# Attention whose short transpositions are done for two heads in one go, and earlier in their step

## The chip, the core and the metric

The kernel runs on one core of a Trainium2 chip. The time is the device time of one execution in microseconds (us). Before the change it is 2401.09 us, the median of 3 runs (2400.51 to 2401.67). The engines are named as the profile names them: PE is TensorE (matrix products and transpositions), PEld its weight loads, ACT is ScalarE, DVE is VectorE, POOL is GpSimd and SP is SyncE, which here issues the transfers.

## The reference

One transformer layer on `x` of shape (2, 1024, 512), in float32. Only the attention bears on the change:

```python
q = rope(hidden @ Wq.T)        # 32 heads of 128, per token
k = [k_c, rope(k_r)]           # 8 key/value heads, from low-rank projections
v = (c_kv @ Wupv.T)            # 8 heads of 128
scores = where(causal, q @ k.T / sqrt(128), -1e9)
attn = softmax(scores, axis=-1)
out = (attn @ v) @ Wo.T        # four query heads share one key/value head
x = layernorm(x + out)
# then a gated feed-forward layer with 4-bit weights, and a second layernorm
```

## The kernel before, in words

Every float32 product is done as three products of a high and a low part (`PASSES`), so each operand is kept as a pair: ACT copies the high part, DVE or POOL subtracts it to get the low part.

The program has three stages: projections of keys, values and latents for all tokens; attention (from 235 to about 2012 us of the span); the feed-forward layer. The attention stage makes 16 turns, one for each pair of a batch entry and a key/value head. Turn 0 is written out ("first"), turns 1 to 14 are a hardware loop ("loop"), turn 15 is written out ("last"), and a short "end" follows.

A turn has 32 steps, and 32 cells: cell c stands for query tile i = c // 4 (128 queries) and head h = c % 4 of the four query heads. In step s:

- PE computes the scores of cell s (`scores`): i+1 key tiles of 128 columns, into one of two PSUM buffers `b_sps`; 3 products for tiles 0 to 3, 6 narrower ones for tiles 4 to 7.
- DVE applies mask and scale and finds the maximum (L1250), into one of four slots of `b_sc` in SBUF. ACT takes the exponential with the row sum (L1026). Two steps later DVE starts its step with the reciprocal of the sum (L1258), and ACT multiplies by it (`normalise`, L1032; it raises `norm_done`).
- Three steps later (`LAG`) PE transposes the cell's probabilities, 128x128 at a time, in pieces of up to four key tiles, into one of two PSUM buffers `b_tps` (`transposes`, L1536). ACT copies the high part of the piece to `b_pt` (`hi_pt`, L1047), DVE subtracts for the low part (`lo_pt`, L1268; it raises `pt_lo`, which frees the PSUM buffer for the piece after next).
- Between these PE does "fill" work in slices of single products: values times probabilities of a query tile (`pv`), output projection (`wo`), and the queries of later cells (`q0`, `q1`). `FILL` and `ROOM` say which and how many products a step takes; `SHARES` cuts a step's fill into shares around the pieces, and `PE_ORDER`, `ACT_ORDER`, `DVE_ORDER` say in which order an engine does the jobs of a step ("0" and "1" are the first and second piece).

In the loop's part between steps 3 and 15 PE does scores, piece 0, fill; from step 16 on it does scores, a share of fill, piece 0, a share, piece 1, the last share. Cells of tiles 0 to 3 have one piece of 1 to 4 key tiles; cells of tiles 4 to 7 have a piece of 4 and a second one of 1 to 4 key tiles: 48 pieces a turn. Each engine works strictly in its own order; a wait on a semaphore holds all that stands behind it.

Two more jobs matter below. A `wo` product writes to one of two PSUM banks, and the next job of the same bank waits until DVE has added the result to `b_ys` (`add_y`, L1279), which DVE does at the start of the step after the product ended. And in steps 22, 26 and 30 of turns 0 to 14 DVE unpacks a piece of the feed-forward weights (L1296 to L1306) at the end of its step.

Of the kernel before, what the change touches and what calls it, by code (L numbers as in the profile page):

```python
# [25 lines left out]
ALU = mybir.AluOpType  # L26
ACT = mybir.ActivationFunctionType
# [3 lines left out]
GQ = HEADS // KV  # L31
# [22 lines left out]

def pieces(c):

    i = c // GQ
    first = c if i < 4 else 16 + 2 * (c - 16)
    out = [(first, 0, min(4, i + 1))]
    if i >= 4:  # L60
        out.append((first + 1, 4, i - 3))
    return out


PIECES = 48

# [31 lines left out]
def part_of(step):  # L98

    return (step >= LAG) + (step >= 16) + (step >= 24)  # L100
# [17 lines left out]

SHARES = ((1,), (0, 1), (1, 1.25, 1))


# [211 lines left out]
def layer(nc, x, xT, wqT, wkrT, wdkT, wupkT, wupvT, woT, w13p, s13p, w2p, s2p, cosT, sinT, shifts,  # L333
# [5 lines left out]
    with ExitStack() as ctx:  # L339
# [109 lines left out]
        def thru(c):  # L449

            return pieces(c)[-1][0] + 1 if c >= 0 else pieces(c + CELLS)[-1][0] + 1 - PIECES

# [475 lines left out]
        def _(act):  # L928
# [106 lines left out]
            def hi_pt(it, c, which):  # L1035
                i, h = c // GQ, c % GQ
                for n, j0, nj in pieces(c)[which:which + 1]:
# [9 lines left out]
                    nc.scalar.activation(pt[:, u % PT_UNITS, HI, 0:nj, h * P:(h + 1) * P], tps[n % 2][:, 0:nj],  # L1047
                                         ACT.Copy)\
                        .then_inc(pt_hi, 1)
# [86 lines left out]

            for _ in range(60):
                act.sem_inc(placed, 1)
# [27 lines left out]
        def _(dve):  # L1166
# [93 lines left out]
            def lo_pt(it, c, which):  # L1260
                i, h = c // GQ, c % GQ
                for n, j0, nj in pieces(c)[which:which + 1]:
# [5 lines left out]
                    nc.vector.tensor_tensor(pt[:, u, LO, 0:nj, h * P:(h + 1) * P], tps[n % 2][:, 0:nj],  # L1268
                                            pt[:, u, HI, 0:nj, h * P:(h + 1) * P], ALU.subtract).then_inc(pt_lo, 1)

# [195 lines left out]
        def _(pe):  # L1466
# [64 lines left out]
            def transposes(it, c, piece):  # L1531
                n, j0, nj = piece
                pe.wait_ge(norm_done, CELLS * it + c + 1)
                pe.wait_ge(pt_lo, PIECES * it + n + 1)
                for j in range(nj):
                    last = nc.tensor.transpose(tps[n % 2][:, j], sc[:, c % S_RING, (j0 + j) * P:(j0 + j + 1) * P],  # L1536
                                               ident[:])
                last.then_inc(t_done, 1)
# [149 lines left out]
            def turn_of(it, turn):  # L1688
                for step in range(CELLS):
# [11 lines left out]
                    shares = cut(parts, SHARES[len(ts)])  # L1701
                    for job in (0, 1, "scores") if step == 0 else PE_ORDER[part_of(step)]:
                        if job == "scores":
# [114 lines left out]
```

## Time and profile before

| | us |
|---|---|
| median of 3 runs | 2401.09 |
| the profiled execution | 2403.64 |
| its span, first to last instruction | 2401.9 |
| PE busy | 2376.6 (99%), 12028 products and transpositions |
| PEld busy | 1993.7 (83%) |
| ACT busy | 1619.4 (67%), 3221 instructions |
| DVE busy | 1428.4 (59%), 3780 instructions |
| POOL busy | 579.1 (24%) |
| mean granted TensorE clock | 0.997 of full |
| attention stage, 235 to 2012 us: PE, ACT, DVE busy | 1768.1, 1460.8, 1198.9 of 1777 |
| PE's share of the chain that ended last | 94% |

The profiled execution took 1.7 us more than its span, and 2.6 us more than the median of the runs. The records of matrix products overlap, since the engine is pipelined, so a busy PE is no proof that nothing waits: a wait is seen as a product that starts later than the rhythm of its neighbours.

### The profile page before, as it was taken

To read this page: it belongs to the slowest core of one execution; us is meant where nothing else is said; L and a number is where in the kernel's file an instruction comes from. 1 tells how busy PE (TensorE), PEld (TensorE's weight loads), DVE (VectorE), ACT (ScalarE), POOL (GpSimd) and SP (SyncE) were. 2 spreads that over 40 slices of the span, in tenths; PEclk is the share of its full clock that TensorE was granted. 3 is DMA by queue.
4 is the path that set the end of the run, shared out by engine and by line. 5 is a ranking of instruction groups with operands and counts; after the bars stand their busy time and mean duration, and the time that the engine had idled before them with its cause. 6 is when DMAs were issued, how large, how long until landed. Compare 5 with 4: busy or idle time off the path is not lost.

```text
span 2401.9 us, 41145 instructions
## 1 busy us (share of the span) xinstructions
PE 2376.6 (99%) x12028; PEld 1993.7 (83%) x12028; DVE 1428.4 (59%) x3780; ACT 1619.4 (67%) x3221; POOL 579.1 (24%) x453
## 2 busy tenths in 40 slices
PE   9999999999999999999999999999999999999998
PEld 7888888888888888888888888888888888888886
DVE  5334666676767666666667666766676675242332
ACT  4223878788888878888878888887878885122211
POOL 3002323233332323232323233232323220000000
PEclk9999999999999999999999999999999999999999
DMA  8868444344353544344434434344444445320110
GB/s 271 289 212 295 139 134 139 127 140 144 133 174 103 175 131 153 127 140 136 152 127 140 137 133 160 120 170 120 161 134 140 132 141 196 131 71 35 52 35 18
DMA packets 133239, 340.24 MB, mean 142 GB/s; under 512 B 13312, under 2 KB 30720, under 8 KB 122624
## 3 DMA queue, kind: packets, MB, share of 16 engines
q1 hardware_dynamic: 133184, 339.53, 41.9%
q8 instruction: 31, 0.51, 0.1%
q14 instruction: 24, 0.20, 0.0%
HBM read 232.00 MB, written 111.67 MB: 143 GB/s over the span
## 4 chain that ended last, share of the span: by engine, by line
PE 94%; DVE 2%; ACT 2%; issue 1%; DMA 0%; POOL 0%; DVEq 0%; SPq 0%; ACTq 0%; POOLq 0%
PE b_ps L267 43%; PE b_sps L267 34%; PE b_tps L1536 10%; PE b_tps L1590 2%; PE b_ps L1590 2%; PE b_tps L267 2%; ACT b_sc L1026 1%; DVE b_ys L1279 0%; DVE b_wraw L1303 0%; DVE b_wraw L1300 0%; DMA b_xs<-xs_d 0%; ACT b_pt L1047 0%; PE b_sps L1545 0%; ACT b_sc L1032 0%; DVE b_pt L1268 0%
## 5 line engine op out<-in xcount | busy, mean ns | idle before, releaser
L1268 DVE TENSOR_TENSOR b_pt<-b_tps,b_pt 128x512 fp32r<-128x512 f32 (+3 forms) x768 | 426.8, 556 | 303.0 <-ACT b_pt L1047 300.0
L267 PE MATMUL b_sps<-b_kt,b_qs 128*128 128x512 f32 (+4 forms) x2304 | 497.2, 343 | 0.7 <-POOL b_qs L878 0.7
L1032 ACT ACTIVATE b_sc<-b_sc,b_rinv 128x896 f32<-128x896 f32 (+7 forms) x512 | 396.1, 774 | 126.5 <-DVE b_rinv L1258 121.1
L267 PEld LDWEIGHTS b_sps<-b_kt,b_qs 128*128 128x128 f32 x2304 | 403.1, 188 | 56.3 <-POOL b_qs L878 1.1
L267 PE MATMUL b_ps<-b_xs,b_wq 128*128 128x512 f32 x1536 | 442.0, 407 | 1.0 <-DMA b_xs<-xs_d 1.0
L1047 ACT ACTIVATE b_pt<-b_tps 128x512 fp32r<-128x512 f32 (+3 forms) x768 | 366.9, 478 | 105.6 <-PE b_tps L1536 103.9
L267 PE MATMUL b_ps<-b_pt,b_vt 128*128 128x512 f32 x1584 | 435.5, 402 | 0.3 <-DVE b_ys L1279 0.3
L267 PE MATMUL b_ps<-b_wo,b_ot 128*128 128x512 f32 x1536 | 425.5, 406 | 6.2 <-DVE b_ys L1279 6.2
L1026 ACT ACTIVATE b_sc<-b_sc,b_nmax 128x896 f32<-128x896 f32 (+7 forms) x512 | 395.6, 773 | 43.8 <-DVE b_nmax L1250 40.0
L1250 DVE CUSTOM_DVE_ANT_0 b_sc<-b_sps,b_mask 128x896 f32<-128x896 f32 (+7 forms) x512 | 386.4, 755 | 15.4 <-PE b_sps L267 15.3
L1536 PE MATMUL b_tps<-b_ident,b_sc 128*128 128x128 f32 x2304 | 374.3, 272 | 1.0 <-DVE b_pt L1268 1.0
L1536 PEld LDWEIGHTS b_tps<-b_ident,b_sc 128*128 128x128 f32 x2304 | 291.8, 140 | 75.5 <-issue 3.8
L267 PEld LDWEIGHTS b_ps<-b_pt,b_vt 128*128 128x128 f32 x1584 | 284.3, 188 | 49.0 <-DVE b_ys L1279 0.5
L267 PEld LDWEIGHTS b_ps<-b_wo,b_ot 128*128 128x128 f32 x1536 | 269.4, 189 | 53.3 <-DVE b_ys L1279 10.8
L267 PEld LDWEIGHTS b_ps<-b_xs,b_wq 128*128 128x128 f32 x1536 | 272.5, 189 | 49.1 <-issue 3.7
L878 POOL TENSOR_TENSOR b_qs<-b_qf,b_qs 128x512 fp32r<-128x512 f32 x124 | 160.3, 1293 | 434.4 <-ACT b_qs L1006 434.4
L267 PE MATMUL b_sps<-c_xs,c_up 128*128 128x512 f32 (+3 forms) x1056 | 247.7, 390 | 0.0
L267 PEld LDWEIGHTS b_sps<-c_xs,c_up 128*128 128x128 f32 (+1 forms) x1056 | 195.2, 185 | 43.7
L874 POOL TENSOR_TENSOR b_sw<-b_sw,b_sin 128x512 f32<-128x512 f32 x128 | 166.0, 1297 | 146.5 <-ACT b_sw L999 145.1
L1327 DVE TENSOR_TENSOR c_hb<-b_sps,c_hb 128x512 f32<-128x512 f32 (+1 forms) x44 | 30.4, 691 | 196.2 <-PE b_sps L267 189.6
L1232 DVE TENSOR_TENSOR b_qf<-b_ps,b_cos 128x512 f32<-128x512 f32 x128 | 88.5, 691 | 96.9 <-ACT b_sw L999 55.0
L887 POOL TENSOR_TENSOR b_wo<-b_wraw,b_wo 128x512 fp32r<-128x512 f32 x64 | 82.9, 1295 | 228.7 <-ACT b_wo L1020 228.7
(133 smaller groups left out, 2278.0 us busy)
## 6 DMA issues: line engine op xcount, KB each, us to landing
b_xs<-xs_d SPq DMA_DIRECT2D x32, 2048.0 KB, 9.2
b_ys<-y_d SPq DMA_DIRECT2D x128, 256.0 KB, 2.7
y_d<-b_ys SPq DMA_DIRECT2D x128, 256.0 KB, 3.0
k_d<-a_ks SPq DMA_DIRECT2D x32, 512.0 KB, 3.9
v_d<-a_vs SPq DMA_DIRECT2D x32, 512.0 KB, 3.0
b_kt<-k_d SPq DMA_DIRECT2D x64, 256.0 KB, 4.5
b_vt<-v_d SPq DMA_DIRECT2D x16, 1024.0 KB, 4.8
b_wraw<-in_wqT SPq DMA_DIRECT2D x64, 256.0 KB, 2.7
```

Source lines behind the costliest of these rows:

```text
L267: ins = nc.tensor.matmul(out, *every[n], start=(n == 0), stop=(n == len(every) - 1))
L874: nc.gpsimd.tensor_tensor(sw[:], sw[:], sinq[:, blk * TB:blk * TB + TB], ALU.mult).then_inc(sin_done, 1)
L878: nc.gpsimd.tensor_tensor(qs[:, blk, h, LO], qf[:], qs[:, blk, h, HI], ALU.subtract).then_inc(q_lo, 1)
L887: nc.gpsimd.tensor_tensor(wo[:, h, LO], wraw[:, h % 2], wo[:, h, HI], ALU.subtract).then_inc(w_lo, 1)
L1026: nc.scalar.activation(sc[:, slot, 0:w], sc[:, slot, 0:w], ACT.Exp, bias=nmax[:, slot:slot + 1], scale=-1.0, accum_out=rsum[:, slot:slot + ...
L1032: nc.scalar.activation(sc[:, slot, 0:w], sc[:, slot, 0:w], ACT.Copy, scale=rinv[:, slot:slot + 1])\
L1047: nc.scalar.activation(pt[:, u % PT_UNITS, HI, 0:nj, h * P:(h + 1) * P], tps[n % 2][:, 0:nj], ACT.Copy)\
L1232: nc.vector.tensor_tensor(qf[:], banks[bk], cosq[:, blk * TB:blk * TB + TB], ALU.mult)\
L1250: nc.vector.tensor_tensor_reduce(out=like_banks(sc[:, slot, 0:w], i), in0=both_banks(sps[c % 2], i), in1=like_banks(mask[:, S - w:S], i), ...
L1268: nc.vector.tensor_tensor(pt[:, u, LO, 0:nj, h * P:(h + 1) * P], tps[n % 2][:, 0:nj], pt[:, u, HI, 0:nj, h * P:(h + 1) * P], ALU.subtract) ...
L1536: last = nc.tensor.transpose(tps[n % 2][:, j], sc[:, c % S_RING, (j0 + j) * P:(j0 + j + 1) * P], ident[:])
L1590: last = nc.tensor.matmul(c_y[t], c_hs[0:w, f % 2, a, t * P:(t + 1) * P], c_w2[f][b][0:w], start=(f == 0 and k == 0), stop=(f == FT - 1 an ...
```

## The change

The pieces of one or two key tiles are no longer made for each head: the odd head's step transposes them for itself and the head before, so that a piece fills two or four of the four places of the PSUM buffer. This concerns query tiles 0 and 1 (their only piece) and 4 and 5 (their second piece). The even heads of tiles 0 and 1 have no piece of their own in their step. A turn has 40 pieces in place of 48, with the same 144 transpositions. In the odd heads' steps PE does the joined piece first, before the scores of that step; tile 4's and 5's steps with a single piece have the fill in one share behind that piece.

```diff
+JOINED = (0, 1, 4, 5)
+def all_pieces():
+    n, out = 0, []
+    for c in range(CELLS):
+        i, two = c // GQ, c % 2
+        mine = [] if i < 2 else [(1, 0, min(4, i + 1))]
+        if i in JOINED and two:
+            mine.insert(0, (2, 0, i + 1) if i < 2 else (2, 4, i - 3))
+        elif i >= 6:
+            mine.append((1, 4, i - 3))
+        out.append([(n + k, *piece) for k, piece in enumerate(mine)])
+        n += len(mine)
+    return out
...
+JOINED_SHARES = (None, (1,), (1, 1))
...
             def transposes(it, c, piece):
-                n, j0, nj = piece
+                n, cells, j0, nj = piece
                 pe.wait_ge(norm_done, CELLS * it + c + 1)
                 pe.wait_ge(pt_lo, PIECES * it + n + 1)
                 for j in range(nj):
-                    last = nc.tensor.transpose(tps[n % 2][:, j], sc[:, c % S_RING, (j0 + j) * P:(j0 + j + 1) * P],
-                                               ident[:])
+                    for e in range(cells):
+                        last = nc.tensor.transpose(tps[n % 2][:, j * cells + e],
+                                                   sc[:, (c - cells + 1 + e) % S_RING,
+                                                      (j0 + j) * P:(j0 + j + 1) * P], ident[:])
                 last.then_inc(t_done, 1)
...
-                    for job in (0, 1, "scores") if step == 0 else PE_ORDER[part_of(step)]:
+                    order = (0, 1, "scores") if step == 0 else PE_ORDER[part_of(step)]
+                    if cell and joined(cell[1]):
+                        order = (0, "scores", "fill", 1, "fill") if len(ts) == 2 else (0, "scores", "fill")
+                        shares = cut(parts, JOINED_SHARES[len(ts)])
+                    elif cell and not ts:
+                        order = ("scores", "fill")
+                    for job in order:
```

`hi_pt` and `lo_pt` take the joined piece as one instruction, 256 columns for each key tile; `thru`, which says how far the transpositions must be before a slot of `b_sc` is written again, counts the joined piece for both of its heads.

PE's order in the loop before, steps 3 and 4 (L1536 transposes, L267 with `b_sps` are the scores, with `b_ps` the fill; the register rows set up waits):

```order
365 L267 MATMUL b_sps<-b_kt,b_qs 128x256 x3
366 L1534 ISA
367 L1536 MATMUL b_tps<-b_ident,b_sc 128x128
368 L267 MATMUL b_ps<-b_xs,b_wq 128x512 x6
369 L1522 REGISTER_ALU
370 L267 MATMUL b_sps<-b_kt,b_qs 128x256 x3
371 L1534 REGISTER_ALU
372 L1536 MATMUL b_tps<-b_ident,b_sc 128x128
373 L267 MATMUL b_ps<-b_xs,b_wq 128x512
```

The same two steps after the change (here L1569 transposes and L289 is every product):

```order
347 L289 MATMUL b_sps<-b_kt,b_qs 128x256 x3
348 L289 MATMUL b_ps<-b_xs,b_wq 128x512 x6
349 L1566 ISA
350 L1569 MATMUL b_tps<-b_ident,b_sc 128x128 x2
351 L1554 REGISTER_ALU
352 L289 MATMUL b_sps<-b_kt,b_qs 128x256 x3
353 L289 MATMUL b_ps<-b_xs,b_wq 128x512
```

Cell 0's transposition left step 3, and both cells' stand ahead of step 4's scores, where cell 1's stood behind them.

PE's order in steps 22 and 23 of the loop before, up to the first `wo` product that needs the bank of the previous `wo`:

```order
488 L267 MATMUL b_sps<-b_kt,b_qs 128x384 x6
489 L267 MATMUL b_ps<-b_wo,b_ot 128x512 x4
490 L1534 REGISTER_ALU
491 L1536 MATMUL b_tps<-b_ident,b_sc 128x128 x4
492 L1634 ISA
493 L1635 REGISTER_ALU
494 L267 MATMUL b_ps<-b_xs,b_wq 128x512 x4
495 L1534 REGISTER_ALU
496 L1536 MATMUL b_tps<-b_ident,b_sc 128x128
497 L267 MATMUL b_ps<-b_xs,b_wq 128x512 x4
498 L1522 REGISTER_ALU
499 L267 MATMUL b_sps<-b_kt,b_qs 128x384 x6
```

After the change, the same place:

```order
454 L1569 MATMUL b_tps<-b_ident,b_sc 128x128 x2
455 L1554 REGISTER_ALU
456 L289 MATMUL b_sps<-b_kt,b_qs 128x384 x6
457 L289 MATMUL b_ps<-b_wo,b_ot 128x512 x4
458 L1668 ISA
459 L1669 REGISTER_ALU
460 L289 MATMUL b_ps<-b_xs,b_wq 128x512 x2
461 L1566 REGISTER_ALU
462 L1569 MATMUL b_tps<-b_ident,b_sc 128x128 x4
463 L289 MATMUL b_ps<-b_xs,b_wq 128x512 x6
464 L1554 REGISTER_ALU
465 L289 MATMUL b_sps<-b_kt,b_qs 128x384 x6
```

Two transpositions now stand ahead of step 22's scores, and the piece of four stands behind six products of fill where it stood behind four.

DVE's order in step 22 after the change; before, the two rows of L1299 were L1268 with 4x128 and then with 128 columns:

```order
468 L1280 ISA b_sc,b_nmax<-b_sps,b_mask 128x768
469 L1280 ISA b_nmax 128x1
470 L1299 TENSOR_TENSOR b_pt<-b_tps,b_pt 128x256
471 L1299 TENSOR_TENSOR b_pt<-b_tps,b_pt 128x4x128
472 L1326 ISA
473 L1332 TENSOR_TENSOR b_wraw<-b_wraw,d_sh 128x512
474 L1335 TENSOR_TENSOR b_wraw<-b_wraw,d_sh 128x512
475 L1337 REGISTER_ALU
476 L1338 TENSOR_TENSOR b_wraw<-b_wraw 128x512
477 L1288 RECIPROCAL b_rinv<-b_rsum 128x1
478 L1309 REGISTER_ALU
479 L1310 REGISTER_ALU
```

The small piece's low part stands ahead of the large one's, and the large one's now stands directly ahead of the unpacking and of `add_y` behind it.

## Rows read from the trace of the kernel before

**Rows 1.** Who TensorE's weight loads waited for: total us, times, longest.
```profile
PEld b_ps L267 <- DVE b_ys L1279: 11.3, 16, 0.7
```
**Rows 2.** Groups by form: busy us, mean ns of one, idle before.
```profile
L1047 ACT ACTIVATE b_pt<-b_tps 128x256 fp32r<-128x256 f32 x128 | 47.5, 371 | 30.4 <-PE b_tps L1536 30.4
L1047 ACT ACTIVATE b_pt<-b_tps 128x128 fp32r<-128x128 f32 x128 | 33.3, 260 | 0.3 <-PE b_tps L1536 0.3
```
**Rows 3.** Instructions in time, turn 6, steps 3 and 4: start us, us, what.
```profile
904.25 0.69 DVE L1268 TENSOR_TENSOR b_pt<-b_tps,b_pt 128x512 fp32r<-128x512 f32 x1
904.47 0.61 PE L267 MATMUL b_sps<-b_kt,b_qs 128*128 128x256 f32 x3
...
904.99 0.33 PE L1536 MATMUL b_tps<-b_ident,b_sc 128*128 128x128 f32 x1
...
905.38 0.69 DVE L1268 TENSOR_TENSOR b_pt<-b_tps,b_pt 128x512 fp32r<-128x512 f32 x1 [0.44 <-ACT b_pt L1047]
...
905.99 0.15 DVE L1258 RECIPROCAL b_rinv<-b_rsum 128x1 f32<-128x1 f32 x1
...
906.18 0.40 ACT L1032 ACTIVATE b_sc<-b_sc,b_rinv 128x128 f32<-128x128 f32 x1 [0.45 <-DVE b_rinv L1258]
...
906.55 0.52 PE L267 MATMUL b_sps<-b_kt,b_qs 128*128 128x256 f32 x3
```
**Rows 4.** The same, steps 4 to 6.
```profile
907.26 0.42 DVE L1250 CUSTOM_DVE_ANT_0 b_sc<-b_sps,b_mask 128x256 f32<-128x256 f32 x1
...
907.73 0.51 ACT L1026 ACTIVATE b_sc<-b_sc,b_nmax 128x256 f32<-128x256 f32 x1
...
908.53 0.27 PE L1536 MATMUL b_tps<-b_ident,b_sc 128*128 128x128 f32 x1
...
908.89 0.42 DVE L1250 CUSTOM_DVE_ANT_0 b_sc<-b_sps,b_mask 128x256 f32<-128x256 f32 x1
...
909.59 0.40 ACT L1032 ACTIVATE b_sc<-b_sc,b_rinv 128x128 f32<-128x128 f32 x1
...
910.49 0.52 PE L267 MATMUL b_sps<-b_kt,b_qs 128*128 128x256 f32 x3
```
**Rows 5.** The same, steps 22 and 23.
```profile
959.27 1.09 PE L267 MATMUL b_ps<-b_wo,b_ot 128*128 128x512 f32 x4
...
960.20 0.60 PE L1536 MATMUL b_tps<-b_ident,b_sc 128*128 128x128 f32 x4
...
960.83 0.60 ACT L1047 ACTIVATE b_pt<-b_tps 128x512 fp32r<-128x512 f32 x1 [1.05 <-PE b_tps L1536]
961.33 0.93 ACT L1026 ACTIVATE b_sc<-b_sc,b_nmax 128x768 f32<-128x768 f32 x1
...
961.46 0.69 DVE L1268 TENSOR_TENSOR b_pt<-b_tps,b_pt 128x512 fp32r<-128x512 f32 x1 [0.87 <-ACT b_pt L1047]
...
962.25 0.27 ACT L1047 ACTIVATE b_pt<-b_tps 128x128 fp32r<-128x128 f32 x1
...
962.75 0.68 DVE L1300 TENSOR_TENSOR b_wraw<-b_wraw,d_sh 128x512 int32<-128x512 int32 x1
...
964.88 0.67 DVE L1279 TENSOR_TENSOR b_ys<-b_ps,b_ys 128x512 f32<-128x512 f32 x1
...
965.60 0.73 PE L267 MATMUL b_ps<-b_wo,b_ot 128*128 128x512 f32 x2 [0.41 <-DVE b_ys L1279]
```
**Rows 6.** The same, turn 0, step 8.
```profile
245.38 0.69 PE L267 MATMUL b_sps<-b_kt,b_qs 128*128 128x384 f32 x3
245.47 0.49 ACT L1032 ACTIVATE b_sc<-b_sc,b_rinv 128x256 f32<-128x256 f32 x1
...
246.01 0.44 PE L1536 MATMUL b_tps<-b_ident,b_sc 128*128 128x128 f32 x2
```
**Rows 7.** The same, turn 15, step 26.
```profile
1976.11 0.94 ACT L1032 ACTIVATE b_sc<-b_sc,b_rinv 128x768 f32<-128x768 f32 x1 [1.26 <-DVE b_rinv L1258]
1976.27 1.38 PE L267 MATMUL b_sps<-b_kt,b_qs 128*128 128x448 f32 x6
```

More of the change, by code:

```diff
@@ L52, with joined @@
 UNITS = 12
-def pieces(c):
[L57 to L65, printed above, removed]
+JOINED = (0, 1, 4, 5)
[11 more added lines that the diff above has]
+    return out
+ALL_PIECES = all_pieces()
+PIECES = sum(len(mine) for mine in ALL_PIECES)
+assert PIECES % 2 == 0
+def pieces(c):
+    return ALL_PIECES[c]
+def joined(c):
+    return any(e == 2 for _n, e, _j0, _nj in pieces(c))
 def unit_of(i, j0):
@@ L449, in thru, with piece_of @@
         def thru(c):
-            return pieces(c)[-1][0] + 1 if c >= 0 else pieces(c + CELLS)[-1][0] + 1 - PIECES
+            here = c % CELLS
+            last = [n for n, _e, _j0, _nj in pieces(here)]
+            if here % 2 == 0 and joined(here + 1):
+                last.append(pieces(here + 1)[0][0])
+            return max(last) + 1 - (PIECES if c < 0 else 0)
+        def piece_of(n, cells, nj):
+            return tps[n % 2][:, 0:nj * cells].rearrange("p (j e) q -> p j (e q)", e=cells)
         def cell_at(step, it, turn):
@@ L1035, in hi_pt @@
             def hi_pt(it, c, which):
-                i, h = c // GQ, c % GQ
-                for n, j0, nj in pieces(c)[which:which + 1]:
+                i = c // GQ
+                for n, cells, j0, nj in pieces(c)[which:which + 1]:
+                    h = c % GQ - cells + 1
                     u = unit_of(i, j0)
@@ L1046, in hi_pt @@
                         act.wait_ge(pv_done, QT * it + tile + 1 + PV0)
-                    nc.scalar.activation(pt[:, u % PT_UNITS, HI, 0:nj, h * P:(h + 1) * P], tps[n % 2][:, 0:nj],
-                                         ACT.Copy)\
+                    nc.scalar.activation(pt[:, u % PT_UNITS, HI, 0:nj, h * P:(h + cells) * P],
+                                         piece_of(n, cells, nj), ACT.Copy)\
                         .then_inc(pt_hi, 1)
@@ L1135, in turn_of @@
                             c_tile_hi(t)
-            for _ in range(60):
+            for _ in range(64):
                 act.sem_inc(placed, 1)
@@ L1260, in lo_pt @@
             def lo_pt(it, c, which):
-                i, h = c // GQ, c % GQ
-                for n, j0, nj in pieces(c)[which:which + 1]:
+                i = c // GQ
+                for n, cells, j0, nj in pieces(c)[which:which + 1]:
+                    h = c % GQ - cells + 1
                     u = unit_of(i, j0) % PT_UNITS
@@ L1267, in lo_pt @@
                             dve.wait_ge(a_v_out[p], 16 * 4 * NBLK + a_OUT0)
-                    nc.vector.tensor_tensor(pt[:, u, LO, 0:nj, h * P:(h + 1) * P], tps[n % 2][:, 0:nj],
-                                            pt[:, u, HI, 0:nj, h * P:(h + 1) * P], ALU.subtract).then_inc(pt_lo, 1)
+                    nc.vector.tensor_tensor(pt[:, u, LO, 0:nj, h * P:(h + cells) * P], piece_of(n, cells, nj),
+                                            pt[:, u, HI, 0:nj, h * P:(h + cells) * P], ALU.subtract)\
+                        .then_inc(pt_lo, 1)
             def lo_ot(it, i, bk):
```

## The prediction, made before the changed kernel was run

> **What bounds the kernel now.** I read the profile in this order: the page's busy times with its chain of work that ended last, the view of who waited for whom, and then the instructions in order of time, turn by turn, for PE, ACT and DVE. On the page the reader sees that PE is busy for 99% of the span, and makes 94% of the chain; ACT (67%) and DVE (59%) are far from full. So work taken off ACT and DVE is worth something only where PE waits for it. In the view of waits the reader is to look for PE and its weight loads alone. Within the attention turns one such wait repeats: the load of a `wo` product waits for DVE's addition to `b_ys`, 16 times, 11.3 us in all [rows 1]. In order of time it sits in step 23 of turns 0 to 14. A second, smaller one doesn't show as idle time, only as a late record: in step 3 of turns 1 to 14 cell 0's transposition waits for the PSUM buffer, until DVE's subtraction of the last-but-one piece ends at 904.94, and starts at 904.99 with a record of 0.33 us in place of the 0.27 us of one that waits for nothing [rows 3, 4]. Everything else on PE in a turn stands in rhythm. What decides this change is therefore not the busy time it saves but what it does to these two waits, and whether joined pieces, which stand earlier in PE's order, must wait for their inputs.
>
> **What the change saves on paper.** 8 pieces a turn go, 128 in all. On PE nothing goes: the 144 transpositions a turn stay, and a transposition costs the same alone or in a row, since a piece of four is 0.60 us long and a single one 0.27 us, so that each further one adds (0.60 - 0.27) / 3 = 0.11 us [rows 4, 5]. ACT saves, on a pair of 128-column copies made one of 256, 2 x 0.260 - 0.371 = 0.15 us [rows 2]; with the pairs of 256 made 512 (taking the 0.60 us record of rows 5: 2 x 0.371 - 0.60 = 0.14 us) that is 8 x 0.15 = 1.2 us a turn, 19 us over 16 turns, and DVE saves about as much. None of it is on PE's path except where a wait ends on it.
>
> The same rows are what the Trainium skill speaks about in Perfetto Trace Analysis, section Optimizing Scalar/DVE Operations: grouping operations saves a fixed overhead each if the engine is saturated, but if ACT and DVE are not saturated and cause bubbles on others, breaking instructions up may let work finish sooner. The first half prices the 19 us as a gain only if ACT were the bound, which its 67% denies; the second half speaks against this change, and it is what I find below, by other rows.
>
> **Term A, step 4, a new wait.** The joined piece of cells 0 and 1 stands at the head of step 4 and needs cell 1 normalised. In turn 6 ACT normalises cell 1 from 906.18 to 906.58; it is released by DVE's reciprocal at 905.99, and this by the subtraction that ran from 905.38 and belongs to step 2's last piece [rows 3]. Nothing of this chain is touched by the change, so 906.58 stands, counted from step 2. PE got to step 4's scores at 906.55 [rows 3]. In the new order cell 0's transposition (0.11) is no longer before it, nor its wait. That wait was: the third score product starts 0.27 to 0.29 us before its record's end at 905.08, so at 904.79, and the next would follow at 904.91; the record starts 0.08 later and is 0.06 longer, 0.14 in all. PE arrives at 906.55 - 0.11 - 0.14 = 906.30. How long it takes from the end of the normalisation to the transposition is shown in turn 0, where one does wait for ACT: 245.47 + 0.49 = 245.96, and the transposition starts at 246.01 [rows 6], 0.05 later; with the 0.06 by which a waiting record is longer, the price is 906.58 + 0.05 + 0.06 - 906.30 = 0.39 us. Against the 0.14 us that goes, A is +0.25 us a turn. Bounds: if the normalisation came as early as it could no longer hold PE, A would be -0.14; if the released wait for two semaphores costs another 0.06, +0.31. Behind the waiting transposition stand the scores of step 4, so mask, exponential and the rest of step 4 come later too; the cell 3 normalisation that step 6's joined piece needs ends at 909.59 + 0.40 = 909.99 before, perhaps 0.35 us later now, against PE's arrival at 910.49 + 0.25 - 0.11 = 910.63 [rows 4]: just in time. At cells 5, 7, 17, 19, 21 and 23 of the loop PE comes a microsecond or more behind the normalisation, and nothing waits.
>
> **Term B, step 23, the old wait grows.** Before, DVE's step 22 ends: high part of the large piece (960.83), exponential (961.33), high part of the single one (962.25), its low part, unpacking from 962.75, addition to `b_ys` 964.88 to 965.55, `wo` at 965.60 [rows 5]. Scores of step 22 end at 959.27, so unpacking starts 3.48 us after them. Now the small piece is done ahead, and the large one is last: from the end of the scores 0.36 to the mask operation (908.53 to 908.89, [rows 4]); 0.96 for it and 0.05 to the exponential (907.26 + 0.42 to 907.73, [rows 4]; the mask operation on 768 columns is 0.96 us long); 0.92 to the high part (961.33 to 962.25, [rows 5]); 0.63 to the low part (960.83 to 961.46); and 0.61 until DVE goes on (905.38 to 905.99, [rows 3]). The sum is 3.53. The transpositions of the large piece are not later than that: a product of fill takes about 0.23 (scores ended 959.27, four of them and then the transposition at 960.20), so 6 x 0.23 of fill and 0.63 to the copy make 2.0 us after the scores, when the exponential ends at 2.3. So the chain is as long as before, +0.05; but the scores themselves end later, by the two transpositions now ahead of them less the one moved out of step 21, 0.11 us. PE reaches the `wo` product with as many transpositions and products done as before. So the wait grows by 0.11 + 0.05 = 0.16 us; I take 0.15. Its bounds: the whole wait of about 0.7 us [rows 1] gone, -0.7; or the chain of exponential and copy another 0.3 later, +0.45. I take +0.15, since each link is a row of the same step.
>
> **The ends.** Turn 0 has other fill and no wait A, but in step 8 PE comes to the joined piece of cells 4 and 5 at 245.38 - 0.22 = 245.16 (cell 4's own piece is gone), and cell 5 is normalised at 245.96 [rows 6]: with 0.11 it holds PE 0.9 us. It held it about 0.15 before, so +0.75; bounds 0 and 0.9. Turn 15 has little fill in its later steps and ACT and DVE are close behind PE: cell 23 is normalised at 1976.11 + 0.94 = 1977.05, while PE comes to step 26 at 1976.27 [rows 7], and the joined piece would hold it 0.9 to 1.1 us; against that the shorter order of ACT in the odd steps gives back part and two present waits of some 0.5 us go. I take +0.4, bounds -0.5 and +1.2. Turn 15 has A as well.
>
> **The sum.** Turns 1 to 14: 14 x (0.25 + 0.15) = 5.6 us. Turn 0: 0.15 + 0.75 = 0.9. Turn 15: 0.25 + 0.4 = 0.65. Together +7.1 us. The span goes from 2401.9 to about 2409.0, the profiled execution from 2403.64 to about 2410.7; against the median of 2401.09 it makes 2408.2 us, and I say 2408.
>
> **Rivals.**
> - *The waits swallow each other* (no change). If the half microsecond of slack that PE has before step 23's wait absorbed what PE loses in step 4, A would cost nothing. It needs a DVE chain in step 22 that is not driven by PE. For it: the wait is longer than A. Against it: every link in rows 5 follows PE's scores within the step, and scores shifted by 0.25 shift all. What remains is B and half of the ends: 15 x 0.15 + 0.8 = 3 us, 2404.
> - *The freed DVE and ACT end the wait for `b_ys`* (faster). Place: step 23 of turns 0 to 14. If the exponential, no longer behind the large piece's copy, starts so early that the large piece's copy and subtraction finish before 962.75, the wait shrinks. It decides from the point where mask, exponential, copy and subtraction take less than 3.48 us from the end of the scores; were they 0.7 us shorter, the wait would be gone: 15 x 0.7 = 10 us, and with step 3's wait of 14 x 0.14 = 2 us gone and A not met, 2401 - 12 = 2389 us. For it: ACT stood idle 1.05 us ahead of the copy at 960.83 [rows 5]. Against it: that idle time is spent waiting for scores and transpositions of the same step, and the mask operation can't start before the scores.
> - *More joined pieces wait* (slower still). Step 6's piece has 0.2 us in hand by my working. If the chain through step 4 is 0.3 us later than I think, it waits every turn, and 16 x 0.3 = 5 us come on top, with the upper ends in turns 0 and 15: 2414.
> - *A colder clock.* The Trainium skill (TensorE: Matmul & The Clock Gate, Part 4) says transposing does not count as PE-busy, so that the clock may not be at its high level. By that rule longer rows of transpositions would be a risk. Here the granted clock is 0.997 of full over the whole span, rows of four and eight transpositions included, and no row grows beyond what stands there already; I give it no chance of its own.
>
> **How the numbers follow.** The forecast has 0.6, the first rival 0.2, the second 0.1, the third 0.1. The range has to reach to the first rival's 2404 and beyond it for the unknown signs of the ends, and to the third's 2414: 2400 to 2414. Its inner part, for the forecast alone, is 2404.5 to 2411. About 0.2% (4.8 us) is what a measurement of this kernel can tell from no change. Slower by more than that is above 2405.9: most of the forecast (0.53) and all of the third rival, 0.63. Within: 0.28. Faster: 0.09.
>
> **What would show it.** In the profile after, in steps 3 and 4 of turns 1 to 14: no transposition in step 3, and in step 4 a piece of two whose record is 0.38 + 0.06 us long and starts 0.05 us after ACT's normalisation of cell 1, about 0.4 us after the rhythm of the products ahead of it; a mean turn of about 0.4 us more. In step 23 the wait for `b_ys` stays, near 0.85 us. In turn 0, step 8, a wait for ACT of close to a microsecond. ACT's busy time falls by about 19 us and nothing comes of it. I am wrong if the wait for `b_ys` is gone or under 0.4 us, if step 4's piece starts in rhythm, or if a turn is no longer than before.

## The result, and the profile after

The changed kernel takes 2414.65 us, the median of 5 runs (2413.94 to 2414.99), against 2401.09 us before (5 runs, 2400.51 to 2401.67). The ratio is 1.0053, with a 95% interval of 1.0041 to 1.0064: slower by 13.6 us. I had said 2408 with a range of 2400 to 2414: the sign was right, the loss was nearly double the 7.1 us that I had worked out, and the time lies 0.65 us above the top of the range. One execution of an experiment below, all_large_behind, took 3808 us at a mean granted clock of 0.581, where all others have 0.997 or 0.998, and is left out of its figures. The changed kernel's profiled execution took 2414.68 us, with a span of 2412.9. That is 11.0 us over the span before; the other 2.6 are that the execution profiled before was itself 2.6 above its median. In the traces 1.1 of them lie ahead of turn 0, and 1.2 in turn 1, where only the execution before lost them.

The page after: engines, then the chain that ended last, by engine.

```profile
PE 2378.8 (99%) x12028; PEld 1993.0 (83%) x12028; DVE 1407.1 (58%) x3652; ACT 1611.9 (67%) x3093; POOL 578.7 (24%) x453
...
PE 79%; issue 8%; ACT 7%; DVE 3%; POOL 1%; DMA 1%; DVEq 0%; ACTq 0%; POOLq 0%; SPq 0%
```

ACT and DVE have 128 instructions fewer each and are 7.5 and 21.3 us less busy, and PE's share of the chain fell from 94% to 79%. The experiments tie that fall to tile 4 with ACT's order as it was: the share is 80% and 82% in j4 and j45, 93% and 94% in j01 and j5, and 97% in j45_large. Who PE waited for, in the view of waits (total us, times, longest); the last row answers to [rows 1]:

```profile
PE b_tps L1569 <- ACT b_sc L1061: 5.0, 17, 0.8
PEld b_tps L1569 <- DVE b_pt L1299: 9.9, 16, 0.7
PEld b_ps L289 <- DVE b_ys L1311: 17.7, 16, 1.3
```

The first two are new (before, no such rows), the third has grown from 11.3 us. In 14 turns the first two are one wait, of the joined piece of step 4, seen on PE and on its weight loads; place A below shows which of the two releasers ended it. To place the loss I compared, in both traces, the start of every step's scores on PE, counted from step 1 of its turn. Median over turns 1 to 14: nothing to step 3; about +0.30 us from step 5 to step 11 and +0.29 from there to step 19 (up to 0.14 more in steps 4, 8 and 10, whose scores have a joined piece ahead of them); +0.33 to step 22; +0.56 at step 23; +0.73 from step 27 to the end of the turn (up to 0.98 in steps 24 to 26). So the loss sits in two places, A and B, as I had it: 0.29 us and 0.44 us. Turns 1 to 14 with 0.73 us each and turns 0 and 15 with 1.3 and 1.5 make 13.0 of the 13.6 us.

**Place A**, turn 6, steps 3 and 4 in order of time (start us, us, what; answers to [rows 3]):

```profile
909.11 0.61 PE L289 MATMUL b_ps<-b_xs,b_wq 128*128 128x512 f32 x2
...
909.46 0.40 ACT L1061 ACTIVATE b_sc<-b_sc,b_rinv 128x128 f32<-128x128 f32 x1 [0.45 <-DVE b_rinv L1288]
...
910.00 0.43 PE L1569 MATMUL b_tps<-b_ident,b_sc 128*128 128x128 f32 x2 [0.27 <-ACT b_sc L1061]
...
910.18 0.60 PE L289 MATMUL b_sps<-b_kt,b_qs 128*128 128x256 f32 x3
```

Cell 1's normalisation ends at 909.86, and the joined piece starts 0.14 us after it (0.13 in each of turns 1 to 14), idle time ahead of it, and the scores behind it. DVE's last subtraction ahead of it ended at 909.36, so DVE, which the view names for the weight loads, had long been done: ACT ended the wait.

**Place B**. First the kernel before, turn 6, step 20 and the start of 21, rows not shown so far:

```profile
954.40 0.94 ACT L1026 ACTIVATE b_sc<-b_sc,b_nmax 128x768 f32<-128x768 f32 x1 [0.39 <-DVE b_nmax L1250]
...
955.34 0.26 ACT L1047 ACTIVATE b_pt<-b_tps 128x128 fp32r<-128x128 f32 x1
...
955.62 0.29 DVE L1268 TENSOR_TENSOR b_pt<-b_tps,b_pt 128x128 fp32r<-128x128 f32 x1 [0.66 <-ACT b_pt L1047]
...
955.83 0.15 DVE L1258 RECIPROCAL b_rinv<-b_rsum 128x1 f32<-128x1 f32 x1
955.91 0.95 DVE L1250 CUSTOM_DVE_ANT_0 b_sc<-b_sps,b_mask 128x768 f32<-128x768 f32 x1
```

And after the change, from step 20 to step 23 (the last rows answer to [rows 5]):

```profile
958.23 0.94 ACT L1055 ACTIVATE b_sc<-b_sc,b_nmax 128x768 f32<-128x768 f32 x1 [0.66 <-DVE b_nmax L1280]
...
959.16 0.58 ACT L1077 ACTIVATE b_pt<-b_tps 128x512 fp32r<-128x512 f32 x1
959.77 0.69 DVE L1299 TENSOR_TENSOR b_pt<-b_tps,b_pt 128x512 fp32r<-128x512 f32 x1 [1.24 <-ACT b_pt L1077]
960.38 0.15 DVE L1288 RECIPROCAL b_rinv<-b_rsum 128x1 f32<-128x1 f32 x1
960.46 0.95 DVE L1280 CUSTOM_DVE_ANT_0 b_sc<-b_sps,b_mask 128x768 f32<-128x768 f32 x1
...
962.70 0.58 ACT L1084 ACTIVATE b_ot<-b_ps 128x512 fp32r<-128x512 f32 x1
...
963.12 1.08 PE L289 MATMUL b_ps<-b_wo,b_ot 128*128 128x512 f32 x4
...
963.32 0.69 DVE L1305 TENSOR_TENSOR b_ot<-b_ps,b_ot 128x512 fp32r<-128x512 f32 x1 [0.64 <-ACT b_ot L1084]
963.93 0.95 DVE L1280 CUSTOM_DVE_ANT_0 b_sc<-b_sps,b_mask 128x768 f32<-128x768 f32 x1
...
964.25 0.73 PE L289 MATMUL b_ps<-b_xs,b_wq 128*128 128x512 f32 x2
...
965.86 0.57 ACT L1077 ACTIVATE b_pt<-b_tps 128x512 fp32r<-128x512 f32 x1
...
966.47 0.69 DVE L1299 TENSOR_TENSOR b_pt<-b_tps,b_pt 128x512 fp32r<-128x512 f32 x1 [1.24 <-ACT b_pt L1077]
967.08 0.68 DVE L1332 TENSOR_TENSOR b_wraw<-b_wraw,d_sh 128x512 int32<-128x512 int32 x1
...
969.20 0.67 DVE L1311 TENSOR_TENSOR b_ys<-b_ps,b_ys 128x512 f32<-128x512 f32 x1
...
969.93 1.20 PE L289 MATMUL b_ps<-b_wo,b_ot 128*128 128x512 f32 x4 [0.70 <-DVE b_ys L1311]
```

In step 20 the small copy behind the exponential has become a large one: from the exponential's start to the reciprocal it was 955.83 - 954.40 = 1.43 us, and is 960.38 - 958.23 = 2.15. In the median of turns 1 to 14 step 21's mask operation then starts 1.75 us after its scores in place of 1.22. In step 22 the mask operation stands behind DVE's `lo_ot` (963.32, the low part of values times probabilities), which waits for ACT's copy (962.70), and that stands behind step 21's exponential. The mask operation starts at 963.93, 0.81 us after the scores ended at 963.12. Then comes the same long sequence again, and unpacking starts 3.96 us after the scores, where it was 3.48 [rows 5].

The late `lo_ot` also holds PE itself in step 22: the first query product (964.25) needs the PSUM bank that `lo_ot` reads, and starts 0.24 us after its end at 964.01. In the median it stands 0.37 us behind the product ahead of it, where 0.23 is the rhythm. That 0.14 is most of the step from +0.33 to +0.56. It adds nothing to the turn by my reading, since PE waits for `b_ys` in step 23 whether it comes there a little earlier or later.

### The profile page after: what moved, and what is told of

The parts are those of the page before. It is cut to its first block, busy times and chain, and to the rows that moved or that the text cites. A ratio compares the mean times of both kernels' runs of the same rounds, so it can differ in the third digit from the quotient of the medians.

```text
span 2412.9 us, 40597 instructions
## 1 busy us (share of the span) xinstructions
PE 2378.8 (99%) x12028; PEld 1993.0 (83%) x12028; DVE 1407.1 (58%) x3652; ACT 1611.9 (67%) x3093; POOL 578.7 (24%) x453
## 4 chain that ended last, share of the span: by engine, by line
PE 79%; issue 8%; ACT 7%; DVE 3%; POOL 1%; DMA 1%; DVEq 0%; ACTq 0%; POOLq 0%; SPq 0%
PE b_ps L289 34%; PE b_sps L289 30%; PE b_tps L1569 8%; PE b_tps L1624 2%; PE b_ps L1624 2%; ACT b_sc L1055 2%; ACT b_pt L1077 2%; PE b_tps L289 2%; ACT b_sc L1061 1%; DMA b_wraw<-in_wqT 1%; POOL b_wq L911 1%; ACT b_ot L1084 1%; ACT b_wo L1049 1%; DVE b_wraw L1335 0%; DVE b_wraw L1332 0%
## 5 line engine op out<-in xcount | busy, mean ns | idle before, releaser
L1299 DVE TENSOR_TENSOR b_pt<-b_tps,b_pt 128x512 fp32r<-128x512 f32 (+2 forms) x640 | 406.5, 635 | 264.2 <-ACT b_pt L1077 259.7
L289 PE MATMUL b_sps<-b_kt,b_qs 128*128 128x512 f32 (+4 forms) x2304 | 508.3, 348 | 0.9 <-POOL b_qs L907 0.7
L289 PE MATMUL b_ps<-b_xs,b_wq 128*128 128x512 f32 x1536 | 432.3, 404 | 0.9 <-issue 0.7
L289 PEld LDWEIGHTS b_sps<-b_kt,b_qs 128*128 128x128 f32 x2304 | 393.5, 188 | 46.7 <-POOL b_qs L907 1.3
L289 PE MATMUL b_ps<-b_wo,b_ot 128*128 128x512 f32 x1536 | 413.1, 400 | 10.6 <-DVE b_ys L1311 10.6
L289 PE MATMUL b_ps<-b_pt,b_vt 128*128 128x512 f32 x1584 | 420.0, 398 | 0.3 <-DVE b_ys L1311 0.3
L1077 ACT ACTIVATE b_pt<-b_tps 128x512 fp32r<-128x512 f32 (+2 forms) x640 | 345.7, 540 | 67.2 <-PE b_tps L1569 64.4
L1569 PE MATMUL b_tps<-b_ident,b_sc 128*128 128x128 f32 x2304 | 353.8, 272 | 6.0 <-ACT b_sc L1061 5.0
L1569 PEld LDWEIGHTS b_tps<-b_ident,b_sc 128*128 128x128 f32 x2304 | 286.8, 140 | 81.3 <-DVE b_pt L1299 9.9
L289 PEld LDWEIGHTS b_ps<-b_pt,b_vt 128*128 128x128 f32 x1584 | 287.9, 188 | 52.1 <-DVE b_ys L1311 0.5
L289 PEld LDWEIGHTS b_ps<-b_wo,b_ot 128*128 128x128 f32 x1536 | 276.1, 188 | 63.0 <-DVE b_ys L1311 17.2
L289 PEld LDWEIGHTS b_ps<-b_xs,b_wq 128*128 128x128 f32 x1536 | 273.5, 189 | 52.8 <-issue 6.7
L289 PE MATMUL b_sps<-c_xs,c_up 128*128 128x512 f32 (+3 forms) x1056 | 247.7, 390 | 0.0
L289 PEld LDWEIGHTS b_sps<-c_xs,c_up 128*128 128x128 f32 (+1 forms) x1056 | 195.2, 185 | 43.7
L922 POOL TENSOR_TENSOR b_wraw<-b_wraw 128x512 fp32r<-128x512 f32 (+2 forms) x45 | 57.6, 1281 | 335.3 <-ACT b_wraw L1097 335.3
```

The lines of the kernel that those rows point to most:

```text
L289: ins = nc.tensor.matmul(out, *every[n], start=(n == 0), stop=(n == len(every) - 1))
L922: nc.gpsimd.tensor_tensor(lo.bitcast(F32R), lo, hi, ALU.subtract).then_inc(d_lo, 1)
L1299: nc.vector.tensor_tensor(pt[:, u, LO, 0:nj, h * P:(h + cells) * P], piece_of(n, cells, nj), pt[:, u, HI, 0:nj, h * P:(h + cells) * P], AL ...
L1569: last = nc.tensor.transpose(tps[n % 2][:, j * cells + e], sc[:, (c - cells + 1 + e) % S_RING, (j0 + j) * P:(j0 + j + 1) * P], ident[:])
```

## The experiments

All runs are of 5 rounds beside the kernel before, whose median was 2401.35 to 2402.59 us in the three sets (2401.99 for j01, j45, j01_behind and after_unpack; 2401.35 for j4, j5, j45_large and before_unpack; 2402.59 for the rest); so ratios are compared, not times. Two distances, taken in every trace as the median over turns 1 to 14, go with them: from the end of step 22's scores (the start of PE's next instruction) to its mask operation, and to the unpacking (`d_unpack`). The two loss columns are the shift of PE's scores against the kernel before, within a turn, from step 1 to 19 and from 19 to 31.

| kernel | ratio (95%) | A, us a turn | B, us a turn | mask op after scores | unpacking after scores |
|---|---|---|---|---|---|
| before | 1 | 0 | 0 | 0.47 | 3.49 |
| the change | 1.0053 (1.0041 to 1.0064) | +0.29 | +0.44 | 0.72 | 3.87 |
| j01 | 1.0029 (1.0018 to 1.0039) | +0.31 | -0.02 | 0.43 | 3.49 |
| j01_behind | 1.0001 (0.9992 to 1.0010) | -0.05 | -0.01 | 0.49 | 3.49 |
| j45 | 1.0025 (1.0014 to 1.0035) | -0.01 | +0.38 | 0.71 | 3.85 |
| j4 | 1.0034 (1.0022 to 1.0046) | +0.01 | +0.48 | 0.72 | 3.86 |
| j5 | 0.9991 (0.9982 to 1.0000) | +0.01 | -0.16 | 0.42 | 3.49 |
| j45_pe_only | 1.0023 (1.0015 to 1.0032) | +0.03 | +0.37 | 0.65 | 3.80 |
| j45_act_only | 0.9984 (0.9975 to 0.9993) | -0.01 | -0.25 | 0.34 | 3.24 |
| before_large | 0.9960 (0.9948 to 0.9973) | 0 | -0.64 | 0.36 | 2.80 |
| j45_large | 0.9948 (0.9934 to 0.9961) | 0 | -0.88 | 0.34 | 2.16 |
| all_large_behind | 0.9946 (0.9934 to 0.9959) | -0.03 | -0.88 | 0.34 | 2.16 |
| after_unpack | 1.0040 (1.0027 to 1.0054) | +0.28 | +0.17 | 0.67 | moved |
| before_unpack | 1.0002 (0.9993 to 1.0011) | -0.01 | +0.01 | - | moved |

**One half of the change at a time.**

```diff
-JOINED = (0, 1, 4, 5)
+JOINED = (0, 1)      # j01; (4, 5) in j45, (4,) in j4, (5,) in j5
```

A tile that isn't joined gets its own pieces in `all_pieces`, as before the change.

> Only tiles 0 and 1 are joined, placed as in the change (ahead of the scores). Theory of two places: the joined piece of step 4 waits for cell 1's normalisation, 0.30 us in 15 turns, and nothing happens in step 23: +4.5 us, 2405.6. The wait for b_ys in step 23 stays at 0.66 us. Rival, each joined piece costs by itself (its row of transpositions or its wider copy): half of the pieces, half of the loss, +6.8 us, 2408. Rival, something common to the program (where the code lies): the whole +13.6 us.

> Only tiles 4 and 5 are joined. Theory of two places: the large piece is last in steps 20 and 22, exponential, copy and subtraction follow each other, and PE loses 0.43 us by step 24 of 15 turns, 6.5 us, with about 1 us in step 8 of turn 0 and 0.8 us in turn 15: +8.3 us, 2409.4; step 4 is as before. Rival, each joined piece costs by itself: +6.8 us, 2408. The two waits feed each other: then this and the kernel with tiles 0 and 1 alone sum to clearly less than 13.6 us.

Measured: 2408.52 and 2408.60 us. By the totals alone the rival "each joined piece costs by itself" had it, half and half. The traces decide otherwise: j01 loses only in step 4 and nothing in step 23, j45 the reverse, each with about the amount that it has in the change. The losses of 0.29% and 0.25% sum to 0.54% against the change's 0.53%, so they neither feed nor swallow each other. In us j01 lost 6.5 and j45 6.6, where I had expected 4.5 and 8.3.

> Only tile 4's second piece is joined (steps 20 and 22). Theory: what PE loses by step 24 comes from the large piece being last in steps 20 and 22, ahead of the exponentials that step 23 needs, so tile 4 alone brings what tiles 4 and 5 bring in the loop, 0.37 us a turn: 15 x 0.37 = +5.5 us, about 2407.5; turn 15 has its +1.2 us at step 24. Rival, each joined piece costs: half of it, +3 us, 2405.

> Only tile 5's second piece is joined (steps 24 and 26). Theory: nothing waits there in the loop, the scores of every step start at the same distance as before: 0 +- 0.05 us a turn, 2401 to 2403. Rival, each joined piece costs: +3 us, 2405.

Measured: 2410.29 and 2399.47 us. The loss is tile 4's, which is what the theory says of steps 20 and 22, but it is 8.9 us against the kernel beside it, larger than the 5.5 expected. Tile 5 gives about 2 us back where I had expected nothing; the interval of the ratio ends at 1.0000, but its trace shows the gain too, 0.16 us a turn, most of it in step 24. Together, 7.0 us, they are near the 6.6 that j45 loses. About 0.10 us of the gain can be placed: in the kernel before, the second query product of step 24 starts 0.33 us behind the first, after a weight load that sat idle (3.7 us in 14 turns in the view of waits, put to "issue"). The 0.33 is in j01 and j4 too; in j5, j45 and the change it is 0.23. My prediction, which had everything else on PE in rhythm, overlooked this small wait.

**A, by place.** j01 with the joined piece where the single one stood:

```diff
-                        order = (0, "scores", "fill", 1, "fill") if len(ts) == 2 else (0, "scores", "fill")
+                        order = (0, "scores", "fill", 1, "fill") if len(ts) == 2 else ("scores", 0, "fill")
```

> Only tiles 0 and 1 are joined, and the joined piece stands behind the scores of its step, where the single one stood. Theory of two places: PE comes 0.6 us later to the piece of step 4, cell 1 is normalised by then, A is gone, and so is the 0.14 us wait of step 3: -2 us, 2399. Rival, a joined piece costs by itself, wherever it stands: +6.8 us, 2408. Rival, the piece moved behind the scores holds up the next step's mask operation: some 0.1 us a piece, 2403 to 2406.

Measured: 2402.12 us, no difference from before. A is gone: joining itself costs nothing, being ahead of the scores does. The gain of 0.14 us in step 3 came only to a third, and 2399, my expectation, was missed by 3 us. Turn 6, step 4:

```profile
904.90 0.40 ACT L1061 ACTIVATE b_sc<-b_sc,b_rinv 128x128 f32<-128x128 f32 x1 [0.45 <-DVE b_rinv L1288]
905.00 0.51 PE L289 MATMUL b_sps<-b_kt,b_qs 128*128 128x256 f32 x3
905.43 0.43 PE L1569 MATMUL b_tps<-b_ident,b_sc 128*128 128x128 f32 x2
```

The piece still starts 0.13 us after the normalisation, with the 0.43 us record of one that waits (0.38 without): even behind the scores PE comes a little early.

**B, by its chain.** j45 and one or both of two edits: PE transposes the large piece straight behind the scores, and ACT copies it ahead of the exponential.

```diff
-JOINED_SHARES = (None, (1,), (1, 1))
+JOINED_SHARES = (None, (1,), (0, 1))          # PE
...
-                    for job in ACT_ORDER[part_of(step)]:
+                    order = ACT_ORDER[part_of(step)]                     # ACT
+                    if (cell := cell_at(step - LAG, it, turn)) and joined(cell[1]) and len(pieces(cell[1])) == 2:
+                        order = ("take", "normalise", 0, 1, "exp", "weights", "q")
+                    for job in order:
```

> Tiles 4 and 5 joined; in the steps of odd heads PE transposes the large piece straight behind the scores, and ACT copies it ahead of the exponential. Theory: then the copy runs beside the mask operation, the exponential is the last link, and the low part is done before it ends; the chain from the scores of step 22 to the unpacking falls from about 4.0 to about 2.6 us, so the added loss goes and most of the old wait of 0.66 us for b_ys with it: below before by 0.4 to 0.66 us in 15 turns, 2392 to 2396. If only the added loss goes: 2402. Rival, the loss is in PE's own rows or in the joined copy: 2408 as for tiles 4 and 5 without this.

> Tiles 4 and 5 joined; PE transposes the large piece straight behind the scores, but ACT still copies it behind the exponential. Theory (the order on ACT makes the chain exponential, copy, subtraction): the large piece has long been transposed when ACT comes to it either way, so the chain from the scores of step 22 to the unpacking stays near 4 us and the time stays at 2408.6 (2407 to 2410). Rival (PE came too late with the large piece): near 2389.

> Tiles 4 and 5 joined; ACT copies the large piece ahead of the exponential, but PE transposes it only behind the first half of the fill, as in the change. Theory: the copy ends at about 2.6 us after the scores and the exponential at 3.55, the low part at 3.3, so unpacking starts about as it did in the kernel before (3.48): the added loss goes, the old wait stays, 2401 (2398 to 2404). Rival (the order on ACT is all that counts): near 2389.

Measured: 2388.86 with both, 2408.09 with PE's alone, 2398.97 with ACT's alone. The last two lie in their expected ranges; in j45_act_only the chain is even 0.25 us shorter than in the kernel before, not only as short. The first gained more than the 2392 to 2396 expected: the chain is 2.16 us in place of the 2.6 I had worked out, and tile 5's gain comes on top. Step 22 of turn 6, first with both:

```profile
952.58 0.60 PE L1572 MATMUL b_tps<-b_ident,b_sc 128*128 128x128 f32 x4
...
952.94 0.96 DVE L1283 CUSTOM_DVE_ANT_0 b_sc<-b_sps,b_mask 128x768 f32<-128x768 f32 x1
953.22 0.60 ACT L1077 ACTIVATE b_pt<-b_tps 128x512 fp32r<-128x512 f32 x1 [0.77 <-PE b_tps L1572]
...
953.94 0.94 ACT L1055 ACTIVATE b_sc<-b_sc,b_nmax 128x768 f32<-128x768 f32 x1
...
954.76 0.68 DVE L1335 TENSOR_TENSOR b_wraw<-b_wraw,d_sh 128x512 int32<-128x512 int32 x1
```

then with PE's alone:

```profile
961.67 0.60 PE L1569 MATMUL b_tps<-b_ident,b_sc 128*128 128x128 f32 x4
...
963.33 0.94 ACT L1055 ACTIVATE b_sc<-b_sc,b_nmax 128x768 f32<-128x768 f32 x1 [0.55 <-DVE b_nmax L1280]
...
964.27 0.58 ACT L1077 ACTIVATE b_pt<-b_tps 128x512 fp32r<-128x512 f32 x1
964.88 0.69 DVE L1299 TENSOR_TENSOR b_pt<-b_tps,b_pt 128x512 fp32r<-128x512 f32 x1 [1.25 <-ACT b_pt L1077]
965.49 0.68 DVE L1332 TENSOR_TENSOR b_wraw<-b_wraw,d_sh 128x512 int32<-128x512 int32 x1
```

With both, ACT copies from 953.22 to 953.82 while DVE's mask operation runs (952.94 to 953.90), and the exponential starts 0.12 us later; unpacking starts 2.18 us after the transposition started. With PE's alone the piece is transposed just as early, lies there for two microseconds until ACT has done the exponential, and unpacking starts after 3.82 us. With ACT's alone the mask operation is back at 0.34 us behind the scores. So the late mask operation of step 22 comes from ACT's order: neither PE's order nor the size of the copy makes it late, once the copy stands ahead of the exponential. In the view of waits of j45_large the 16 waits for `b_ys` have become one, of 0.3 us on PE and 0.5 us on its weight loads, in turn 15.

**The order without joining.**

```diff
-                    shares = cut(parts, SHARES[len(ts)])
+                    shares = cut(parts, (0, 1, 1) if step in (20, 22, 24, 26) else SHARES[len(ts)])
```

> The kernel before, nothing joined; in steps 20, 22, 24 and 26 PE transposes the large piece straight behind the scores, the rest of the fill behind it in two halves, the single piece last but one. ACT and DVE as before. Theory (the gain is one of order, not of joining): the large copy runs beside the mask operation, exponential from 1.37 to 2.3 us after the scores, then the single piece, unpacking at 2.9 in place of 3.48: the wait for b_ys falls from 0.66 to about 0.1 us, 15 x -0.56 = -8 us, 2393. Rival (it needs the small piece out of the way, as joining does): 2401.

Measured: 2392.91 us. Three quarters of the gain (0.40% of 0.52) need no joining: in this kernel ACT copies the large piece ahead of the exponential already, and only PE delivered it late (1.05 us idle in [rows 5]). Joining adds 0.24 us a turn. Unpacking then starts 2.16 us after the scores in place of 2.80, but that isn't where it comes from, since before_large has no wait for `b_ys` in step 23 either. Before_large loses 0.15 us in step 20, where its weight loads wait for DVE's subtraction to free a PSUM buffer (12 times, 4.0 us in all); j45_large doesn't.

**The unpacking out of the way.** In the change (after_unpack) and in the kernel before (before_unpack):

```diff
                             for bk, kind, a, g in finished(step, turn, 1):
                                 take(bk, kind, it + g, a)
+                            if turn in ("first", "loop") and step - 1 == D_SPLIT[0]:
+                                d_unpack(it, 0)
...
-                    if turn in ("first", "loop") and step in D_SPLIT:
+                    if turn in ("first", "loop") and step in D_SPLIT[1:]:
```

> The changed kernel, with DVE's unpacking of step 22 moved behind the addition to b_ys of step 23. Theory: what is lost in step 23 is lost through the chain exponential, copy, subtraction, unpacking, addition; without the 2.1 us of unpacking in it, the old wait of 0.66 us and the added 0.43 us both go in 15 turns: 2414.6 - 16 = 2398. A and the losses of turns 0 and 15 stay. Rival, PE's loss in steps 22 and 23 comes from elsewhere (the query product's bank, the pieces themselves): only the old wait goes, 10 us, 2404.6. Rival, the wait moves on into steps 24 and 25, since the mask operation of step 23 stands behind the unpacking: 2408 to 2414.

> The kernel before, with the unpacking of step 22 behind the addition to b_ys of step 23 and nothing joined. In the changed kernel this ended the wait for b_ys, but PE then waited in step 24 for the bank of a query product, because DVE's mask operation of step 23 came 2 us later. If the wait moves in the same way here, -1 to -3 us net, 2399 to 2401; if it doesn't, 15 x 0.66 = -10 us, 2392.

Measured: 2411.31 and 2401.64 us. My expectation of the first, 2398, failed, and its second rival held; the second gained nothing where I had expected 1 to 3 us. Step 24's scores do start 0.68 us earlier than before in before_unpack, and by step 25 it is all given back. In after_unpack, turn 6:

```profile
966.88 0.95 DVE L1280 CUSTOM_DVE_ANT_0 b_sc<-b_sps,b_mask 128x768 f32<-128x768 f32 x1
...
970.69 0.69 DVE L1262 TENSOR_TENSOR b_qf<-b_ps,b_cos 128x512 f32<-128x512 f32 x1 [2.18 <-ACT b_sw L1028]
...
971.51 1.19 PE L289 MATMUL b_ps<-b_xs,b_wq 128*128 128x512 f32 x4 [0.35 <-DVE b_qf L1262]
```

The mask operation stands behind the unpacking, the exponential and ACT's copies of a query behind it, and PE's next query product needs the bank that they read. Taking the 2.1 us out of one wait puts them into the next; shortening the chain, as j45_large does, is another thing than moving a link.

**The whole change, repaired.** Both orders in the kernel with all four tiles joined:

> All four tiles joined as in the change, with both repairs: the joined piece of tiles 0 and 1 behind the scores, and the large piece of tiles 4 and 5 straight behind the scores and copied ahead of the exponential. Theory: the parts add, -12.5 us for tiles 4 and 5 and 0 for tiles 0 and 1: 2389 (2387.5 to 2390.5). Rival, the waits feed each other: 2392 or more.

Measured: 2389.73 us (2387.42 to 2390.74), about as j45_large and inside the range expected. Both are 0.5% faster than the kernel before and 1.0% faster than the change. Joining tiles 0 and 1 adds nothing to the gain.

## Why the prediction was right in sign and short in size

- *What bounds the kernel.* Right: 29 us less busy time on ACT and DVE brought nothing, and what counted were two waits of PE. Of the sizes, DVE's 21.3 us fit; ACT's copies out of `b_tps` fell by 21.2 us as I had it (366.9 to 345.7 by their groups), but its busy time by only 7.5 and not 19. ACT's records overlap (the exponential at 961.33 starts while the copy of 960.83 runs to 961.43 [rows 5]), and with 128 instructions fewer this overlap fell by 14.5 us too, from 204.6 to 190.1 over the span.
- *Term A*, +0.25 us a turn, measured +0.29. The place, the releaser and the record of the piece (0.43 us for 0.44) were right; the piece starts 0.13 us after the normalisation, not the 0.05 I took from turn 0 (where it is again 0.06 after the change). The 0.14 us that were to go against it went only to a third in j01_behind. The margins behind it held: no other joined piece waits for a normalisation in turns 1 to 14, so the third rival is refuted, and that its 2414 is the time measured is chance.
- *Term B*, +0.15, measured +0.43: this is the step that failed. It failed at "from the end of the scores 0.36 to the mask operation", which I had taken from step 5, where DVE stood idle for 0.62 us until the scores ended. I had written that each link is a row of the same step; this one, the mask to the exponential and the last one were not. In step 22 it is 0.72 in the median (0.47 before), because DVE is still busy with `lo_ot` there. I had counted the large piece in its new place once, in step 22, and not in step 20, although the change does the same there; that lengthens step 20 (1.43 to 2.15 us in turn 6), and DVE and ACT carry it through step 21. That step 20 is where it begins is read from the traces; no run changes step 20 without step 22. That ACT's order is the cause, the runs show: with it changed, the distance is 0.34, and the chain 3.24 us in j45_act_only and 2.16 in j45_large; with PE's alone it stays at 0.65 and 3.80. In sum, the chain is 3.87 - 3.49 = 0.38 us longer in place of 0.05, and the scores come 0.04 later in place of 0.11: 0.42 for my 0.16. The missing 0.28 us a turn are 15 x 0.28 = 4.2 us of the 6.5 that the sum fell short. My bound of +0.45 just held it.
- *The ends.* Turn 0 lost 1.3 us from step 1 to 31 (said: 0.9). Step 8's scores came 0.65 us later (its piece waits for ACT, below), but 0.3 of that came back in the next step. About 0.5 came in step 21, in the three kernels with all four tiles joined (nothing in j45, and 0.14 over steps 20 and 21 in j01): there PE waits 0.31 us with its piece of four until DVE has subtracted the joined piece. Why it needs all four stays open. Turn 15 lost 1.5 (said 0.65). Of these 0.9 are in step 2, at its first query product, which waits for nothing the profile shows; of the fourteen traces j01 and j45_large have about the same, all others don't, all_large_behind and after_unpack with the same four tiles joined among them, so nothing ties it to the change. The remaining 0.58 is A (0.1) and the piece ahead of step 24's scores, which waits 0.85 us for ACT; the one of step 26, which I had named, starts right behind its normalisation (0.05 us) and hardly waits, and 0.8 us comes back there.

Turn 0, step 8, after the change (answers to [rows 6]):

```profile
244.04 0.49 ACT L1061 ACTIVATE b_sc<-b_sc,b_rinv 128x256 f32<-128x256 f32 x1
...
244.59 0.66 PE L1569 MATMUL b_tps<-b_ident,b_sc 128*128 128x128 f32 x4 [0.31 <-ACT b_sc L1061]
...
245.00 0.77 PE L289 MATMUL b_sps<-b_kt,b_qs 128*128 128x384 f32 x3
```

The piece starts 0.06 us behind the normalisation, the scores behind the piece.

- *The signs I had named.* A turn is 0.76 us longer from one to the next in the median, not 0.4; the wait for `b_ys` is 1.14 us and not 0.85; step 4's piece starts 0.13 us after the normalisation and not 0.05; in turn 0, step 8, the weight loads wait 0.7 us and PE 0.31, not close to a microsecond. None of the signs of being wrong appeared.
- *The rivals.* Waits did not swallow each other (the halves add). "The freed DVE and ACT end the wait for `b_ys`" asked for a chain under 3.48 us from scores to unpacking; in the change it is 3.87, and where an experiment made it so (2.16) the time fell to 2389, which is what that rival gave. Its condition was not met in the change. That its sum fits is partly luck: its 10 us for the wait are there, but the other 2 us it took from step 3's wait, which j45_large still has; there about as much comes from tile 5's steps. The granted clock is 0.998, and no row grew with the length of a series of transpositions.
- *The Trainium skill*, Perfetto Trace Analysis, section Optimizing Scalar/DVE Operations: its second half, that breaking instructions up may let work finish sooner where ACT and DVE aren't saturated, points the way the time went. The runs don't bear it out as the cause: j01_behind (1.0001) and j45_large (0.9948) have instructions as large, which only stand elsewhere, and lose nothing.

What remains open: the rest of what tile 5 gives back (0.06 us a turn), why turn 0's wait in step 21 needs all four tiles joined, and 0.5 us between the change's 13.6 and the sum of its halves' medians (6.5 and 6.6 above the kernel before), which is within the intervals.

## What to carry to other kernels

Making two small instructions into one moves something: ask which piece is now the last of its step, and follow the sequence of exponential, copy and subtraction through every step that has it, not only the one in front of the known wait. A long copy out of PSUM belongs beside an operation of the other engine that is running anyway (here the mask operation), ahead of the one that depends on it; it then cost nothing here, and that needed both orders, PE's and ACT's. And take a link's duration from a row of the step it is used for: the distance from the scores to the mask operation was 0.36 us in one step and 0.72 in another.

## What the runs showed of the hardware

One distance that I had not reckoned with, from the end of what PE waits for to PE's start. In turns 1 to 14, where PE waits, it is always 0.05 or 0.06 us for the `wo` product behind `add_y`, 0.13 us for step 4's joined piece behind the normalisation, and 0.24 or 0.25 us for step 22's query product behind `lo_ot`. The first has no further wait behind the one that held it, the second has one for another semaphore, the third two. In turn 6 the sequencer's records of the third stand at 964.05, 964.16 and 964.24 after `lo_ot` had ended at 964.01: each further wait took about 0.1 us, and only after the one that held it had passed. In turns 0 and 15, which are written out and not a loop, a piece with the same two semaphores starts 0.05 or 0.06 us after the normalisation. No run varied the number of waits by itself, or their order. The sizes came as read from before: ACT's copy of 256 columns is 368 ns long in the mean after the change, all of them with two heads side by side, against 371 with one [rows 2].
